# Cross attention: probabilities times values in two pieces per half batch, and the value projection shifted half a batch

## The reference, cut to what matters

```python
q = x @ Wq.T + bq                      # 16 x 64 x 256
k = context @ Wk.T + bk                # 16 x 1601 x 256
v = context @ Wv.T + bv
# 16 heads of width 16
scores = jnp.einsum('bhtd,bhcd->bhtc', q, k) / jnp.sqrt(d)
attn = jax.nn.softmax(scores, axis=-1)
out = jnp.einsum('bhtc,bhcd->bhtd', attn, v)
```

## Time and profile before

| what | value |
|---|---|
| median of three runs | 4626.18 us |
| span of the profiled execution | 4638.8 us |
| PE busy | 3918.2 us, 84% |
| DVE busy | 2215.6 us, 48% |
| ACT busy | 1766.8 us, 38% |
| POOL busy | 680.3 us, 15% |
| mean granted TensorE clock | 0.915 of full speed |

### The profile page before, as it was taken

The page is one execution under the profiler, slowest core; times in us unless marked ns, Lnnn a source line. Parts: engine busy times, 40 slices in busy tenths (PEclk is TensorE's granted clock), DMA queues, the critical chain, the costliest instruction groups (busy, mean ns, idle before and its releaser), DMA issues. The chain is left out here.

```text
span 4638.8 us, 142149 instructions
## 1 busy us (share of the span) xinstructions
PE 3918.2 (84%) x64206; PEld 3075.8 (66%) x64206; DVE 2215.6 (48%) x4131; ACT 1766.8 (38%) x3676; POOL 680.3 (15%) x393
## 2 busy tenths in 40 slices
PE   7999998744995499999966889999963789999988
PEld 5777776533774288888734567777742668878865
DVE  4545554442443455555464355555525255555533
ACT  3444444210221244544422345445432244444431
POOL 1111110123002311111040011111103011111100
PEclk9999999766998699999987899999976899999988
DMA  2111210023996211111030111111013611111100
GB/s 81 52 62 65 65 56 28 17 76 103 343 350 226 85 39 39 39 40 44 12 92 20 31 51 39 44 38 38 31 27 114 210 60 39 39 39 39 33 10 32
DMA packets 109046, 330.32 MB, mean 71 GB/s; under 512 B 31680, under 2 KB 55760, under 8 KB 101632
## 3 DMA queue, kind: packets, MB, share of 16 engines
q1 hardware_dynamic: 98800, 299.61, 19.5%
q0 software_dynamic: 6912, 18.88, 1.3%
q10 hardware_dynamic: 2736, 2.75, 0.2%
HBM read 261.80 MB, written 51.00 MB: 67 GB/s over the span
## 5 line engine op out<-in xcount | busy, mean ns | idle before, releaser
L657 DVE TENSOR_REDUCE x_pm<-banks 128x4 f32<-128x1536 f32 (+2 forms) x512 | 935.4, 1827 | 694.1 <-PE banks L558 694.1
L759 ACT ACTIVATE x_pl<-banks 128x384 f32<-128x384 f32 x1536 | 628.8, 498 | 744.5 <-PE banks L541 744.4
L481 POOL TENSOR_TENSOR x_cl<-xnT,x_ch 128x1601 fp32r<-128x1601 f32 x116 | 386.3, 3330 | 2215.0 <-ACT x_ch L774 2215.0
L764 ACT ACTIVATE x_kT<-banks,x_bk 128x384 f32<-128x384 f32 (+2 forms) x512 | 305.1, 596 | 537.8 <-PE banks L569 537.8
L581 PE MATMUL banks<-x_wh,x_ch 128*128 128x256 f32 (+1 forms) x1664 | 490.8, 295 | 0.0
L541 PE MATMUL banks<-x_q,x_kT 32*128 32x128 f32 x13312 | 482.3, 277 | 4.3 <-issue 4.0
L558 PE MATMUL banks<-x_kT,x_q 32*128 32x384 f32 (+2 forms) x4096 | 459.0, 513 | 14.1 <-DVE x_v L689 9.0
L581 PE MATMUL banks<-x_wh,x_cl 128*128 128x256 f32 (+1 forms) x1664 | 469.0, 282 | 0.0
L581 PE MATMUL banks<-x_wl,x_ch 128*128 128x256 f32 (+1 forms) x1664 | 467.6, 281 | 0.0
L569 PE MATMUL banks<-x_ch,x_wh 128*128 128x384 f32 (+2 forms) x1024 | 410.8, 401 | 44.9 <-DVE x_cl L740 44.1
L541 PEld LDWEIGHTS banks<-x_q,x_kT 32*128 32x128 f32 x13312 | 436.6, 185 | 7.1 <-issue 4.5
(11 more groups left out here) (369 smaller groups left out, 5484.5 us busy)
## 6 DMA issues: line engine op xcount, KB each, us to landing
xnT<-in_ctxT SPq DMA_DIRECT2D x120, 800.5 KB, 4.4
e_w<-in_L_pack SPq DMA_DIRECT2D x127, 608.0 KB
e_w<-in_L_pack SPq DMA_DIRECT2D x21, 1154.0 KB
routed_x<-x_zero SPq DMA_DIRECT2D x16, 1024.0 KB, 9.1
e_xt<-routed_x SPq DMA_DIRECT2D x16, 1024.0 KB, 7.8
routed_y<-e_y SPq DMA_DIRECT2D x32, 512.0 KB, 7.5
a_swap<-a_raw SPq DMA_DIRECT2D x64, 128.0 KB, 2.3
actT<-in_ctxT SPq DMA_DIRECT2D x8, 800.5 KB, 4.3
```

The source lines that it names most:

```text
L481: nc.gpsimd.tensor_tensor(cl[:, u, k, 0:CTX], staged(b, k), ch[:, u, k, 0:CTX], ALU.subtract).then_inc(low_done, 1)
L657: nc.vector.tensor_reduce(pm[:, c, :, g], src[:, :, 0:hi - lo], AX.X, ALU.max).then_inc(max_done, 1)
L759: nc.scalar.activation(probabilities(c, j, lo, hi).rearrange("p t q -> p (t q)"), mine[j][:, 0:(hi - lo) * P], ACT.Exp).then_inc(exp_done, 1)
L764: nc.scalar.activation(kT[:, c, lo:hi], mine[1 if g == 0 and inside(b if c else b - 1) else 0][:, 0:hi - lo], ACT.Identity, bias=col[:, c: ...
```

## The change

P times V of a half is cut by tiles rather than by heads: `weigh` does tiles 0 to 6 (56 matmuls) in the cycle with g = 2 of the same half, and tiles 7 to 12 (48 matmuls) in the cycle with g = 0 that follows. Each piece forms its own sum in bank 0; DVE copies the first to SBUF (`acc`) and adds the second to it. So every even cycle has one P times V piece. The values are projected in eight pieces instead of seven, four cycles (half a batch) later than the keys of the same cycle number, and ahead of the keys' piece rather than behind it. The sums cross partitions by a shuffle on DVE instead of a matmul on PE, so the matmul with `swap` goes. DVE now works out numerator and sums once per batch from SBUF (four instructions of 128 x 128), and divides after. ACT makes the high part of the context in cycles (1,0) and (1,2) rather than (0,2) and (1,2), and ahead of the key copy. The context has one more buffer, and SP starts the transfer into it one step earlier (`low_done` 2b + k + 3 instead of + 4).

```diff
-    VALUE_TILES = [(0, 2), (2, 4), (4, 6), (6, 7), (7, 9), (9, 11), (11, 13)]
-    VALUES = len(VALUE_TILES)
-    EARLY = GROUPS[0][1]
+    VALUE_TILES = [(0, 1), (1, 3), (3, 5), (5, 7), (7, 8), (8, 10), (10, 11), (11, 13)]
+    FIRST = GROUPS[1][1]
+    PARTS = [(0, FIRST), (FIRST, KEY_TILES)]
...
-        early_p = net.sb(tag + "_pe", [P, 2, 4, EARLY, P], ctx=mem)
-        late_p = net.sb(tag + "_pl", [P, 4, KEY_TILES - EARLY, P], ctx=mem)
+        first_p = net.sb(tag + "_pe", [P, 4, FIRST, P], ctx=mem)
+        second_p = net.sb(tag + "_pl", [P, 4, KEY_TILES - FIRST, P], ctx=mem)
...
-        raw_v = early_p[:, 0].rearrange("p j t q -> p (j t q)")[:, 0:KC * D].rearrange("p (c f) -> p c f", c=KC)
-        raw_c = [buf[:].rearrange("p c n -> p (c n)")[:, 0:CTX] for buf in (net.xnT, net.actT)]
+        raw_v = first_p[:].rearrange("p j t q -> p (j t q)")[:, 0:KC * D].rearrange("p (c f) -> p c f", c=KC)
+        even_raw, first_raw = (buf[:].rearrange("p c n -> p (c n)")[:, 0:CTX] for buf in (net.xnT, net.actT))
...
+        def weighed(k):
+
+            return k % 2 == 0 and 0 <= k // 2 - 1 < 2 * B * KC
+
...
-            sp.wait_ge(low_done, 1)
             load_context(1, 1)
             sp.wait_ge(low_done, 2)
             load_context(1, 0)
...
                 for k in range(KC):
-                    sp.wait_ge(low_done, 2 * b + k + 4)
+                    sp.wait_ge(low_done, 2 * b + k + 3)
                     load_context(b + 2, k)
...
+            def weigh(k):
+
+                half, part = (k // 2 - 1) // 2, (k // 2 - 1) % 2
+                u, c, bank = half // KC % 2, half % KC, sets[k % 2][0]
+                lo, hi = PARTS[part]
+                for e in range(2):
+                    for t in range(lo, hi):
+                        w = P if t < KEY_TILES - 1 else LAST_KEYS
+                        for j in range(4):
+                            at = (4 * c + j) * WINDOW + 16 * e
+                            last = nc.tensor.matmul(bank[32 * j:32 * j + 32, e * S:(e + 1) * S], v[0:w, u, t, at:at + 32],
+                                                    probabilities(j, t, t + 1)[0:w, 0, e * S:(e + 1) * S],
+                                                    start=(t == lo), stop=(t == hi - 1))
+                last.then_inc(pv_full, 1)
+
+            def project_v(k):
+                n = k + 4
+                u, bank = n // CYCLES % 2, sets[k % 2][value_bank(k)]
+                if n == 0:
+                    pe.wait_ge(wv_low, 1)
+                lo, hi = VALUE_TILES[n % CYCLES]
+                for t in range(lo, hi):
+                    w = P if t < KEY_TILES - 1 else LAST_KEYS
+                    for c in range(KC):
+                        for m, (x, y) in enumerate(((ch, wh), (cl, wh), (ch, wl))):
+                            last = nc.tensor.matmul(bank[0:w, (t - lo) * D:(t - lo + 1) * D], x[:, u, c, t * P:t * P + w],
+                                                    y[:, 1, c, :], start=(c == m == 0), stop=(c == KC - 1 and m == 2))
+                last.then_inc(v_full, 1)
...
-            def cycle(b, u, c, g):
-                k = CYCLES * b + 4 * c + g
-                half = 2 * b + c
...
-                        pe.wait_ge(v_taken, VALUES * pb + VALUES)
-                    attend(pu, 1 - c, 0, mine[0])
-                    first = 1
-                if inside(b + 1):
-                    if inside(b):
-                        pe.wait_ge(exp_done, 4 * k + 1 + first)
-                    project_k(b + 1, 1 - u, c, g, mine[first])
-                if first:
-                    attend(pu, 1 - c, 1, mine[0])
-                if g == 3 and inside(b + c):
-                    if inside(b):
-                        pe.wait_ge(exp_done, 4 * k + 4)
-                    pe.wait_ge(z_ready, half + 2)
-                    nc.tensor.transpose(mine[3][:, 0:P], z[:].rearrange("p j r -> p (j r)").bitcast(F32),
+            def cycle(k):
+                if compared(k - 1):
+                    pe.wait_ge(max_done, k + 5)
+                elif k - 2 >= -CYCLES:
+                    wait_copied(k - 2)
+                if scored(k):
+                    scores(k)
+                if compared(k):
+                    wait_copied(k - 1)
+                    maxima(k)
+                if weighed(k):
+                    wait_exp(k, 1)
+                    if not scored(k):
+                        pe.wait_ge(exp_done, 4 * TOTAL)
+                    if not compared(k):
+                        pe.wait_ge(v_taken, min(k + 4, TOTAL))
+                    weigh(k)
+                if valued(k):
+                    wait_exp(k, 1 + value_bank(k))
+                    project_v(k)
+                if shifted(k):
+                    wait_exp(k, 4)
+                    pe.wait_ge(z_ready, k // 4 + 2)
+                    nc.tensor.transpose(sets[k % 2][3][:, 0:P], z[:].rearrange("p j r -> p (j r)").bitcast(F32),
                                         net.ident[:]).then_inc(z_turned, 1)
-                if g == 1 and c == 0 and inside(b - 1):
-                    if inside(b):
-                        pe.wait_ge(exp_done, 4 * k + 4)
-                    pe.wait_ge(o_taken, 4 * half)
-                    nc.tensor.matmul(mine[3][:, 0:KC * S], net.swap[:], den[:].rearrange("p c s -> p (c s)"), start=True,
-                                     stop=True).then_inc(den_full, 1)
-                piece = value_piece(b, u, c, g)
-                if piece and inside(piece[0]):
-                    if inside(b):
-                        pe.wait_ge(exp_done, 4 * k + 2 + first)
-                    project_v(*piece[1:], mine[1 + first])
-
-            def one(b, u):
-                for c in range(KC):
-                    for g in range(4):
-                        cycle(b, u, c, g)
+                if keyed(k):
+                    wait_exp(k, 1 + key_bank(k))
+                    project_k(k)
 
             pe.wait_ge(wk_low, 1)
             pe.wait_ge(pad_set, 2)
             pe.wait_ge(shift_set, 2 + masked)
             pe.wait_ge(sums_set, 2)
-            each_batch(one)
+            for k in range(-CYCLES, TOTAL + 1):
+                cycle(k)
 
         @block.vector
         def _(dve):
-            def take_max(b, u, c, g, src, cycle_no):
-                unit = cycle_no + 5
+            def take_max(k):
+                unit = k + 5
+                b, c, g = place(unit)
                 lo, hi = KEYS[g]
                 dve.wait_ge(m_full, unit + 1)
-                nc.vector.tensor_reduce(pm[:, c, :, g], src[:, :, 0:hi - lo], AX.X, ALU.max).then_inc(max_done, 1)
+                nc.vector.tensor_reduce(pm[:, c, :, g], net.quads[1 - k % 2][:, :, 0:hi - lo], AX.X, ALU.max).then_inc(max_done, 1)
                 if g < 3:
                     return
...
+            def take_weighed(k):
+                n = k // 2 - 1
+                half, part = n // 2, n % 2
+                c, bank = half % KC, sets[k % 2][0]
+                mine = acc[:, c].rearrange("p e s -> p (e s)")
+                dve.wait_ge(pv_full, n + 1)
+                if part == 0:
+                    if half >= KC:
+                        dve.wait_ge(o_step, 6 * (half // KC))
+                    nc.vector.tensor_copy(mine, bank[:, 0:2 * S]).then_inc(o_taken, 1)
+                else:
+                    dve.wait_ge(o_taken, n)
+                    nc.vector.tensor_tensor(mine, bank[:, 0:2 * S], mine, ALU.add).then_inc(o_taken, 1)
...
+            def part_sums(b):
+
+                own, rest = net.parity[:, 12:13], net.parity[:, 13:14]
+                sums = den[:].rearrange("p (c s) -> p c s", c=KC)
+                dve.wait_ge(o_taken, 4 * b + 4)
+                if b:
+                    dve.wait_ge(out_ready, b)
+                nc.vector.tensor_scalar(num[:], acc[:, :, 0], own, None, ALU.mult).then_inc(o_step, 1)
+                nc.vector.tensor_scalar(sums, acc[:, :, 0], rest, None, ALU.mult).then_inc(o_step, 1)
+                dve.wait_ge(o_step, 6 * b + 1)
+                nc.vector.scalar_tensor_tensor(num[:], acc[:, :, 1], rest, num[:], ALU.mult, ALU.add).then_inc(o_step, 1)
+                dve.wait_ge(o_step, 6 * b + 2)
+                nc.vector.scalar_tensor_tensor(sums, acc[:, :, 1], own, sums, ALU.mult, ALU.add).then_inc(o_step, 1)
+
+            def divide(b):
+                dve.wait_ge(o_step, 6 * b + 4)
+                nc.vector.stream_shuffle(rec[:, 0], den[:], [lane ^ 16 for lane in range(32)]).then_inc(o_step, 1)
+                dve.wait_ge(o_step, 6 * b + 5)
+                nc.vector.reciprocal(rec[:, 1], rec[:, 0]).then_inc(o_step, 1)
...
+            def cycle(k):
+                b, c, g = place(k)
+                if compared(k):
+                    take_max(k)
+                if weighed(k):
+                    take_weighed(k)
+                if valued(k):
+                    take_v(k)
+                if b >= 1 and c == 0 and g == 0:
+                    part_sums(b - 1)
```

(14 more changed lines are left out.)

280 lines of the change are left out of this document (99 added, 181 removed).

## The result

The changed kernel takes 4449.74 us (median of four runs, 4443.48 to 4455.40) against 4624.44 for the kernel before (four runs, 4619.70 to 4634.62). The ratio is 0.9624, with a 95% interval of 0.9606 to 0.9641: 174.7 us faster. The forecast was 4490, the range 4430 to 4575.

What follows compares the result with a forecast made beforehand. PE was taken as the bound, busy for 84% of the span. Savings of 14 + 31 + 46 + 20 + 24 = 135 us from a median of 4626.2 gave 4491, forecast as 4490 us, range 4430 to 4575.

Steps and rivals of the forecast that it cites:

- rival 2: PE's instruction stops before P times V vanish entirely: all 90 us go, giving 4447 us; chance 0.14.
- Matmul with swap: On PE, once per batch: dropping the 0.24 us matmul 60 times in the four windows saves 14 us.
- Scores wait less for copies: PE between scores and maxima: waits for copies go, saving 23 us unmasked and 8 masked, 31 together.
- Stops in P times V: PE's idle time before P times V, read as waiting for instructions: smaller blocks save 46 of 90 us.
- Start of a stage: First key matmul to first score: half the values leave this stretch, saving 5 us per stage, 20 in all.
- End of a stage: Last batch: values fill PE's idle time and a smaller P times V piece ends it; 6 us per stage, 24 saved.
- the stops stay: PE's stops before P times V remain, so 46 us of the saving is missing: 4537 us; chance 0.27.
- rival 4: ACT's keys' copy becomes the last wait, delaying maxima and next scores: slower, 4669 us at 0.5 us delay; chance 0.05.

Runs made afterwards that it cites:

- before_after_pv: Kernel before, with each context transfer (and layer 0's zeros) also waiting on SP for the half's P times V: 4502.1 us, ratio 0.9743 to the kernel before.
- sp_order_after_pv_b: Changed kernel, masks' transfer behind the first context transfer, layer 0's zeros later, context transfers also waiting for P times V: 4429.7 us, ratio 0.9536 to before.
- keys_first: Changed kernel with the keys' piece ahead of the values' piece again, ACT taking keys before the shift: 4483.5 us, ratio 0.9703 to the kernel before.
- pv_whole: Changed kernel with P times V of a half as one block of 104 matmuls at g = 0: 4646.1 us, ratio 1.0046 to the kernel before.
- pv_halves_b: Changed kernel with P times V as two 52-matmul blocks per g = 0 cycle, keys' piece between: 4572.2 us, ratio 0.9839 to the kernel before.
- before_again: The kernel before, unchanged, profiled once more: 4604.9 us (one run).
- before_values_first_banks: Kernel before with the values' piece ahead of the keys' piece on PE and their banks exchanged: 4828.9 us, ratio 1.0446 to the kernel before.

## Why the prediction was right, and where it was not

The forecast of faster, in the range of 4430 to 4575, held; it was 40 us short. By number the result lies outside the forecast's own 4465 to 4515 and next to rival 2 (4447), whose mechanism did not come: 29.6 us of the stops stayed, as forecast (25 to 45), and the surplus came from the waits, the last batches and the spread of single runs. Its terms, against the kernels with and without stops (before_after_pv and sp_order_after_pv_b hardly have any):

- **Matmul with swap, 14 us:** right, 13 by the quiet batch, 12 by the medians. The shuffle costs nothing one can see, though my count on DVE was wrong: nine small instructions a batch are new, not six, against eight gone, and the shuffle shows as two records, so DVE has 605 in the third window instead of 577. Its busy time there is 355.73 us after 355.79, not 1 us a batch less.
- **Scores wait less for copies, 31 us: under-sized.** Without stops the windows go from 2595.8 to 2533.4, 62.4 us; less 13 for the matmul that is 49, of which 32 unmasked (I had 23) and 17 masked (I had 8). Keys_first gives 26 of it back, by the order of the pieces with ACT's alone; the rest I put down to P times V, whose copies no longer stand before maxima, but no run has that part alone. I counted each wait by its length; in (0,3) of keys_first maxima that were 0.24 us late made the cycle 0.35 us longer. The masked third was a guess, and low.
- **Stops in P times V, 46 us: right in size.** With stops the windows were 105.1 us longer than without (2700.9 less 2595.8), after the change 57.5: 47.6 gone. I had put the whole at 90 and the gain in the wrong layers: layer 0 gave 34 to 38 us, layer 2 9 or 10, layers 1 and 3 about 2 each, where 12.5 and 17.6 stay. I said that the rest would be mostly in layer 0; 13.0 of 29.6 us are in layer 3. What I had missed is SP's order in masked layers: the wait for the masks holds back the first context transfer until it runs beside the second, at (0,0). That most stops sit in (0,0) was right. My reading that PE waits for its instructions was right too, with two numbers off: the context's second transfer is issued some 3 us before (0,0) in the unmasked layers, not 1, and a packet of q8 goes with 252 records of PE and PEld (128412 over 510), not 279, for I had divided the records of all engines. And the rate inside a block was not all that counts, nor a transfer beside it: a block of 104 stops PE without one (pv_whole).
- **Start of a stage, 20 us: wrong, 9 came.** The values' move gave 14 (3.5 at each, I had 4.2), but the new order took 6: PE waits 2.0 us for a copy of values that DVE does only behind its chain on the last maxima, besides the 2.3 and 1.4 that I had. In that chain stands the CAST that POOL's subtraction holds up, 6.3 us in sum, which I had put at nothing.
- **End of a stage, 24 us: 29 to 33 came,** 33.2 to 35.1 us each, inside what I gave. Taken back alone, the values' place is worth 12.6 and P times V in pieces 28 (pv_whole, 25 in pv_halves_b); the two overlap, so they do not add up.

That is 13 + 49 + 48 + 9 + 29 = 148 us of profiles, where the forecast had 135, and the runs show 175. Most of the other 27 us are the spread of single executions. The profiled runs of before_again (4604.9) and of the changed kernel (4455.4) differ by 149.5 us, which the terms cover; the first lies 17.3 us under the median of the kernel before beside it (4622.2), the second 5.7 over its own (the chips may differ). Where in the program the runs without a profile take these 23 us, no trace shows.

**Rivals.** That the stops stay fell: 29.6 us of 71.2 are left, though layer 3 alone would have borne it out. Two lines on SP remove 105 us of windows from the old kernel, and the 43 stops over 0.5 us all end just behind a packet of q8, so they are PE waiting for instructions, in the old kernel behind data. The Trainium skill ("Runtime: NRT & Kernel Launch", section "Instruction fetch mechanics") says that crossing a block's boundary is mostly hidden. The traces agree as to the number, 43 stops over 0.5 us on 423 packets before; what is not hidden cost 105 us. That PE holds 2048 instructions, as the same section says, no run here shows. That the stops vanish came only with SP's order changed as well. The keys' copy as last wait did not come in the changed kernel; before_values_first_banks suggests how near it was, at 207 us in the old layout, if ACT's own order had not been changed along. I had costed those moves at nothing, and named ACT's queue only in rival 4.
